# The step with C22 behind the sixth product of the next group, together with the sixth step, instead of behind the fifth product with the fourth step

## What is computed

```
attn_out  = softmax((x Wq)(x Wk)^T * scale) (x Wv) Wp + bp
cms_out   = gelu(attn_out cW1 + cb1) cW2 + cb2 + onehot(code)
modifier  = gelu([attn_out, cms_out] mW1 + mb1) mW2 + mb2      # hidden size 2048
y         = clip(x + cms_out + modifier, 0, 1)
out       = layernorm(y + (gelu(y Wdown[s] + bdown[s]) Wup[s] + bup[s])) * ln_w[s] + ln_b[s]
```

## Time and profile before

| | us |
|---|---|
| median of 3 runs | 1055.6 |
| lowest, highest | 1055.45, 1055.94 |
| the profiled execution's own time | 1056.31 |
| span in its profile, first to last instruction | 1054.5 |
| TensorE busy | 1047.5 |
| VectorE busy | 722.5 |
| GpSimd busy | 587.6 |
| ScalarE busy | 473.1 |

### The profile page before, as it was taken

How to read it: one execution, slowest core, us unless ns; L and a number is a source line. 1 busy time by engine, 2 the same in 40 slices (tenths; PEclk the granted TensorE clock), 3 DMA queues, 4 the chain that set the end, 5 groups by cost and what they waited for, 6 DMA issues and landing times.

```text
span 1054.5 us, 13654 instructions
## 1 busy us (share of the span) xinstructions
PE 1047.5 (99%) x4675; PEld 867.3 (82%) x4675; DVE 722.5 (69%) x1020; ACT 473.1 (45%) x901; POOL 587.6 (56%) x577
## 2 busy tenths in 40 slices
PE   9999999999999999999999999999999999999998
PEld 7888888888888888888888888888887888888886
DVE  3735263396555555655688888886697888887868
ACT  3545445454333432433454534444544444333765
POOL 0565774641340531522688977766897876673406
PEclk9999999999999999999999999999999999999999
DMA  7456730101122232111153444344866433335834
GB/s 280 137 165 208 230 110 1 60 1 46 67 83 95 86 120 76 44 62 31 40 185 115 134 118 133 112 125 122 335 217 216 133 120 121 106 114 172 327 81 160
DMA packets 88212, 134.10 MB, mean 127 GB/s; under 512 B 7376, under 2 KB 53200, under 8 KB 87632
## 3 DMA queue, kind: packets, MB, share of 16 engines
q1 hardware_dynamic: 87568, 132.18, 37.7%
q10 hardware_dynamic: 576, 1.05, 0.3%
HBM read 98.34 MB, written 34.87 MB: 126 GB/s over the span
## 4 chain that ended last, share of the span: by engine, by line
PE 93%; DVE 3%; DMA 2%; issue 1%; ACT 0%; POOL 0%; SPq 0%; DVEq 0%; ACTq 0%; POOLq 0%
PE bank L926 31%; PE bank L927 30%; PE bank L928 30%; DMA piece_raw<-adapter_dram 1%; DVE c_T_f L1588 1%; PE bank L1149 1%; PE bank L983 1%; DMA acc<-xT_dram 1%; DVE acc L1732 0%; DVE acc L1665 0%; PE bank L952 0%; DMA y_kept<-acc 0%; DVE H_lo L1640 0%; SPq L516 0%; DVE u_t L1654 0%
## 5 line engine op out<-in xcount | busy, mean ns | idle before, releaser
L721 POOL TENSOR_TENSOR left_x<-rawX,left_x 128x256 fp32r<-128x256 f32 x144 | 131.8, 916 | 156.4 <-ACT left_x L1211 156.3
L1665 DVE TENSOR_TENSOR acc<-bank,acc 128x512 f32<-128x512 f32 x136 | 91.9, 687 | 49.5 <-PE bank L928 49.1
L1724 DVE TENSOR_TENSOR acc<-bank,acc 128x512 f32<-128x512 f32 x166 | 107.0, 683 | 17.0 <-PE bank L928 14.6
L926 PE MATMUL bank<-H_hi,W_hi 128*128 128x512 f32 x304 | 118.5, 390 | 0.0
L928 PE MATMUL bank<-H_hi,W_lo 128*128 128x512 f32 x304 | 118.4, 390 | 0.0
L927 PE MATMUL bank<-H_lo,W_hi 128*128 128x512 f32 x304 | 118.4, 390 | 0.0
L926 PE MATMUL bank<-x_T_hi,left_x 128*128 128x512 f32 x256 | 99.9, 390 | 0.1
L928 PE MATMUL bank<-x_T_hi,left_x 128*128 128x512 f32 x256 | 99.7, 390 | 0.0
L927 PE MATMUL bank<-x_T_lo,left_x 128*128 128x512 f32 x256 | 99.7, 390 | 0.0
L1654 DVE TENSOR_TENSOR u_t<-bank,s_t 128x512 f32<-128x512 f32 x64 | 44.0, 688 | 78.7 <-PE bank L928 76.6
L721 POOL TENSOR_TENSOR left_c<-rawC,left_c 128x256 fp32r<-128x256 f32 x96 | 90.6, 944 | 2.5 <-ACT left_c L1211 2.5
(11 more groups left out here) (224 smaller groups left out, 2825.9 us busy)
## 6 DMA issues: line engine op xcount, KB each, us to landing
ring<-w_kept SPq DMA_DIRECT2D x91, 256.0 KB, 2.7
rawX<-mW_dram SPq DMA_DIRECT2D x16, 512.0 KB, 4.0
rawC<-mW_dram SPq DMA_DIRECT2D x16, 512.0 KB, 4.9
w_kept<-mod_hi SPq DMA_DIRECT2D x7, 896.0 KB, 4.4
w_kept<-mod_lo SPq DMA_DIRECT2D x7, 896.0 KB, 7.3
xT_raw<-xT_dram SPq DMA_DIRECT2D x4, 1024.0 KB, 8.7
x_raw<-x_dram SPq DMA_DIRECT2D x4, 1024.0 KB, 6.1
rawX<-cW_dram SPq DMA_DIRECT2D x8, 512.0 KB, 3.7
```

Source lines behind the costliest of these rows:

```text
L721: pool.tensor_tensor(dst, src, f32(hi), ALU.subtract).then_inc(done, 1)
L926: pe.matmul(tile, sh, mh, start=first_one and n == 0, stop=False, skip_group_check=joined_group)
L1665: op = dve.tensor_tensor(dst, src, dst, ALU.add)
L1724: dve.tensor_tensor(dst, src, dst, ALU.add).then_inc(summed, 1)
```

## The change

S4 (the step with C22) goes from behind P4, where it stood with S3, to behind P5, where it stands in front of S5. TensorE then runs P0 P1 S0 S1 P2 P3 S2 P4 S3 P5 S4 S5 P6 S6 in the 13 groups. Nothing else is edited.

```diff
                     for n, i in enumerate(order_of(g)):
                         if g > MOD0 + 1 or n > 1:
                             product_part(g, i, sources)
-                        for j in {1: (0, 1), 3: (2,), 4: (3, 4), 5: (5,), 6: (6,)}.get(n, ()):
+                        for j in {1: (0, 1), 3: (2,), 4: (3,), 5: (4, 5), 6: (6,)}.get(n, ()):
                             block_step(g - 1, j)
```

## The result

The changed kernel takes 1057.65 us (median of 19 executions, 1056.65 to 1059.81), the kernel before, run beside it, 1055.55 (19 executions, 1054.70 to 1056.41). The ratio is 1.0023, with a 95% interval of 1.0016 to 1.0030. The medians are 2.10 us apart, and the ratio makes it 2.4. The prediction called less than about 0.2%, or 2.1 us, "the same", and the result lies on that line: the interval reaches to both sides of it. The range (1055.9 to 1058.3) held the median; the forecast's own range (1056.5 to 1057.5) did not.

A forecast was written before the change was run, and what follows sets the result against it. TensorE was taken to bound the kernel. Terms of 12 x 0, +1.36 for group 25 and 0 for the rest summed to +1.36, a median of 1057.0 us (own range 1056.5 to 1057.5, full range 1055.9 to 1058.3).

The forecast's parts named there:

- What bounds the kernel: Stretch of the change: TensorE is the bound, reordering its matmuls gains nothing, except possibly in group 25, where it stalls.
- The cover of P5: Twelve groups: U3 ends 0.20 to 0.25 us before P5's weight load needs it, so each costs 0.
- rival 2: U3 late in twelve groups, delaying P5's first weight load: 1060.9 us, or 1057.8 at half that lateness; chance 0.10.
- What waits for S4: VectorE's adds and JC21 unmoved, ScalarE's C21 0.1 us later, SyncE's ring load 2.72 later but covered: cost 0.
- Group 31: W2's low part ready at about 992.4, against its weight load at 992.47: cost 0, at most 0.5 us.
- Rival 3: The end pays too: W2's low part at its longest gives 1057.5 us, another adapter slip 1058.0; chance 0.12.
- Group 25: P5 waits for late U3, S4 no longer fills that wait: cost +1.36 us, one step.
- rival 1: In group 25 x lands early enough that P5 hardly waits: 1055.6 to 1056.1 us, or a gain; chance 0.08.

The follow-up runs named there:

- e1: Changed kernel, but group 25 keeps the old order (new order in the other 12 groups): 1056.00 us, ratio 1.0003 to the kernel before.
- e9: Changed kernel, with join U3 of group 25 made ahead of the adds of S2, run a second time: 1055.23 us, ratio 0.9994 to the kernel before.
- e10: Kernel before, with the new order and join U3 ahead of the adds of S2 in group 25 alone: 1055.07 us, ratio 0.9995.
- e3: Changed kernel, with join U3 of group 25 made ahead of the adds of S2, first run: 1055.10 us, ratio 0.9995 to the kernel before.
- e8: Changed kernel, with VectorE copying 320 columns ahead of join U3 in the 12 groups other than 25: 1058.90 us, ratio 1.0039 to the kernel before.
- e7: Changed kernel, with VectorE copying 64 columns ahead of join U3 in the 12 groups other than 25: 1057.56 us, ratio 1.0018 to the kernel before.
- e11: Changed kernel, with S3 also behind P5 in group 25 (stall one step longer), second run: 1060.07 us, ratio 1.0040 to the kernel before.
- e6: Changed kernel, with six unused matmuls between S3 and P5 of group 25, filling most of the stall: 1057.43 us, ratio 1.0013 to the kernel before.
- e2: Kernel before, with the new order in group 25 alone: 1057.70 us, ratio 1.0023 to the kernel before.
- e4: Kernel before (old order), with join U3 of group 25 made ahead of the adds of S2: 1055.78 us, ratio 1.0002.
- e5: Changed kernel, with S3 also behind P5 in group 25 (stall one step longer), first run: 1059.60 us, ratio 1.0036 to the kernel before.

## Why the prediction was right where it was, and where it failed

**What bounds the kernel; nothing to gain but group 25's stall.** Right. The twelve groups are indifferent to the order (e1, and e9 against e10), and the only gain that the runs found lies in group 25 (e3, e9, e10 together).

**The cover of P5, 12 x 0.** Right: U3 0.20 us behind S3's start in all twelve, 0.24 us to the weight load in group 20, no gap. That the wait holds the weight load too, which set the bound at 0.2 to 0.25 instead of 0.47, is shown by e8: U3 some 0.4 late costs, where 0.47 of cover would have hidden it. The price past the bound was too high, though: rival 2 charged all lateness beyond 0.2 us, which for e8's join makes 0.2 us in each group, and e8 paid 0.11. Rival 2 itself did not come: the joins took 676 to 692 ns as before, and VectorE was idle ahead of U3 in each of the twelve groups, so nothing held it. What the prediction drew against the change from the Trainium skill ("SBUF — State Buffer", "Who interferes with whom") did not bite here.

**What waits for S4, 0.** Right to 0.1 us. JC21 stands at 664.84 on the old scale, predicted 664.8. ScalarE in group 20, C22 and C21:

```profile
663.63 0.72 ACT L1324 ACTIVATE H_hi<-u_t,bias 128x512 fp32r<-128x512 f32 x1 [1.57 <-PE bank L928]
...
664.89 0.72 ACT L1324 ACTIVATE H_hi<-s_t,bias 128x512 fp32r<-128x512 f32 x1
```

C22 now waits for TensorE, as predicted at 664.3 on the old scale (663.63 + 0.66), and C21 comes at 665.55, 0.03 later than in the earlier trace rows; 0.1 was predicted.

**Group 31, 0.** Right, and as close as worked out. GpSimd's low part of W2, and the weight load that waits for it:

```profile
990.40 2.40 POOL L721 TENSOR_TENSOR W_lo<-W_raw,W_hi 128x1024 fp32r<-128x1024 f32 x1 [1.95 <-ACT W_hi L1218]
```

```profile
992.86 0.19 PEld L926 LDWEIGHTS bank<-H_hi,W_hi 128*128 128x128 f32 x1
```

Ready at 992.80, used at 992.86: 0.06 us to spare, where the prediction had 992.4 against 992.47. Rival 3 did not come.

**Group 25, +1.36.** The mechanism was right: one stall, charged to U3, none at S4, and the step behind it undone. From P4 to P6 it took 11.40 us in the profile (812.21 less 800.81). The prediction's 813.18 less 801.47 is 11.71, and U3 was 0.30 sooner. (The 3.17 us of which rival 1 speaks are VectorE's wait for x in the earlier trace rows.) The step that failed is "Cost +1.36, one step": an idle TensorE was priced at its idle time alone. The prediction noted a full clock before and carried it over to the kernel after. The runs show a second price. In 5 of 19 executions the time lies in the upper heap, and the one profiled execution of such a heap (e7) has the granted clock at half behind the stall, which costs about 1.6 us there. Between the means of the two heaps of the changed kernel lie 2.2 (1059.5 and 1057.3). That is the missing term: five nineteenths of 2.2 us are 0.6 in the mean, and without the upper heap the median would be 0.4 lower, which is more than half of the 0.65 by which it missed the forecast. The old stalls, of 0.3 us each, never did it.

That the range held is in part luck. Its upper end, 1058.3, was left for rivals 2 and 3, and neither came; what used the room was a cost that the prediction did not have.

The Trainium skill tells of the same behaviour in "TensorE: Matmul & The Clock Gate", "HAM oscillation — how this bites in real kernels": gaps in which TensorE waits, there for a DMA and 3 to 5 us long, let the chip halve its clock for the work behind them. The traces of e7 and e11 agree that it happens, with 0.51 and 0.50 granted behind stalls of 2.0 and 3.3 us, though e7's stall is shorter than the waits that the page shows. The prediction left this out; a rival "the clock falls in group 25" with 1.6 to 2 us would have moved some chance to slower.

**What stays open.** The lower heap stands 1.7 us above the kernel before (medians 1057.27 and 1055.55), and e6 1.4. The forecast was 1.36 and the profile of group 25 gives 1.05, but that profile has the shortest stall: with the new order group 25 loses 1.88, 1.96 and 2.22 in the profiles at full clock (the changed kernel, e2, e8), with the old one 0.83 and 0.70 (before, e1), so the difference is 1.05 to 1.5 by the pair that is taken. What is left, some 0.2 to 0.3, wasn't explained, nor why the lower heap is split in two. The 2.2 between the heaps is also more than the 1.6 of the slow stretch. Both profiles with a fall belong to executions whose clock became full late (6.3 and 6.8 us), which by itself makes an execution longer; that this is the rest is not shown.

## What to carry to other kernels

Before pulling a matmul forward, ask what its operand hung on in the one place where the schedule is out of step: twelve groups had 0.24 us to spare, and the thirteenth waited for a DMA that its operand didn't even need, through VectorE's order. Mend that order first; behind it the new order is the better one. And price an empty wait of TensorE above its length: behind one of 2 us the clock may fall. A long wait that can't be avoided may be better filled than left empty; e6 speaks for it with 11 executions, and splitting one was not tried.

## What the runs showed of the hardware that was not expected

- With a stall of TensorE of 1.7 to 2.1 us, 14 of 46 executions lie in an upper heap, by their times (the changed kernel 5 of 19, e2 5 of 11, e7 2 of 11, e8 2 of 5). One of the 14 was profiled, e7's, and it has a stretch at half clock behind the stall; that the other 13 have one is inferred. In the profile of the changed kernel TensorE had been busy since 731.6 without a gap of even 0.05 us when the stall came. With 0.7 us of it left empty (e6, 11 executions), with stalls of 0.3 (before, 94; e1, 11) or 0.34 (e4, 11) and with none (e3, e9, e10, 33), no execution lies in such a heap.
- The mean clock alone does not tell the heaps apart. The profiled execution of e8 has 0.998 and no fall in the middle: its stretch at half clock is the last 3.3 us, when TensorE has finished. All 14 executions of the upper heaps have 0.997 or 0.998, but so have four of the kernel before and three of e6.
- The same kernel can have the stall with the clock at 1.00 (e5) and at 0.50 behind it (e11).
- A weight load that comes 0.20 us late leaves its own matmul in time and delays the next by 0.09; behind a real stall the second matmul comes 0.33 to 0.34 behind the first instead of 0.227. A restart costs 0.1 us.
